# Three exponentials ahead of each pair of silus, GpSimd's products no longer held, and chunk 1's first fills spread: a Mamba + SwiGLU kernel

## The chip, the cores and the metric

One core of one Trainium2 chip. The metric is device time in microseconds (us) of one execution, the median of the runs shown; lower is better.

## The reference

The layer is a Mamba block and a SwiGLU block, each followed by a layer norm over a residual sum. The input has 4 sequences of 2048 tokens, model width 256; the inner width is 512, with 16 states per channel.

```python
x_in, res = jnp.split(x @ W_in, 2, axis=-1)
x_conv = silu(_causal_dw_conv(x_in, conv_w, conv_b))
dt, Bm, Cm = jnp.split(x_conv @ W_x, [DT_RANK, DT_RANK + N_STATE], axis=-1)
delta = softplus(dt @ W_dt + b_dt);  A = -exp(A_log)
def step(h, inp):            # along time, for each channel and state
    dA_i, dBu_i, C_i = inp   # exp(delta*A), delta*B*u, C
    h = dA_i * h + dBu_i
    return (h, einsum('bdn,bn->bd', h, C_i))
x = layernorm(x + (y + x_conv * D) * silu(res) @ W_out)
x = layernorm(x + (silu(x @ wg.T) * (x @ wu.T)) @ wd.T)
```

## The kernel before

The 8192 tokens are cut into 16 chunks of 512. Chunk after chunk, a step of 64 **beats** runs the selective scan: beat `b` handles state `b // 4` of channel block `b % 4`, a tile of 128 channels by 512 tokens. A beat needs three things: ScalarE's exponential `da` (function `exp`, line 1094), GpSimd's product `dbu` = `du` times `brep` (`times_b`, line 1237), and VectorE's scan over them (`scan`, line 1432), which makes `h`. TensorE turns `h` to tokens by channels in two halves (`turn_upper`, `turn_lower`, line 737). ScalarE weighs the upper half by C into `gt` (`weigh`, line 1103) and TensorE turns that back into `y_upper` (line 762); VectorE sums the lower half into `acc` (line 1444). The bank `ht_upper` is free for TensorE's next turn only when `gt` is read from it.

All else is fitted between the beats. While chunk i is scanned, the front of chunk i+1 (`xin`, `conv`, `res`, `dtb`, `ct`, `dt`) and the back of chunk i-1 (`o`, `x1t`, `gate`, `up`, `down`) run: TensorE's **fills** into two spare banks at the beats of the table `FILL_AT`, and the reads of them at the beats of `READ_AT`. A table `BEAT` places the rest. Each engine's queue is in the order of these beats, and runs in order; semaphores tie the queues. Chunk 1's front runs in step 0 at beats of its own (`EARLY_FILL`, `EARLY_READ`).

Silu and exponential lie in different tables of ScalarE, so the silus of a step are gathered in two **windows**, each between two table loads (lines 1167 and 1179). `BEAT["silu uz"]` = [31, 32]: the silu of u (next chunk) and of z. `BEAT["silu gate"]` = [43, 45]: the two halves of the gates' silu (line 993); the product with them is VectorE's `kb<-fill` (line 1354), one for each of `up0` to `up5`. Step 0 has z's silu in place of the gates'.

For the beats of a window the exponentials are made in front of it: `AHEAD` = 2 of them, for beats 32, 33 and 44, 45. They go to the buffer `da_ahead`, in SBUF, where all other `da` alternate between two PSUM banks and so wait for the scan two beats before. The exponential of the beat behind these comes after the window.

`HOLD` = (2, 3) delays one product of GpSimd for each window. A product normally waits for the scan four beats before it (`DBU` = 4 buffers). Product 34 waits for the scan of beat 33 instead of 30, and product 47 for beat 45 instead of 43:

```python
used = beat - DBU if beat >= DBU else max(b for b in range(NH) if b % DBU == beat) - NH
after(pool, h_ready, i * NH + max(used, HELD.get(beat, used)) + 1)
```

Scans of most beats have one tile operand in PSUM (`da`) and one in SBUF (`dbu`); those of a window have both in SBUF.

Of the kernel before, what the change touches and what calls it, by code (L numbers as in the profile page):

```python
# [45 lines left out]
FILL_BANKS = 2  # L46


EARLY_FILL = {"xin0": (0, 0), "xin1": (1, 1), "xin2": (2, 2), "xin3": (3, 3), "conv0": (5,), "conv1": (8,),
              "conv2": (11,), "conv3": (14,)}  # L50
EARLY_READ = {"xin0": 1, "xin1": 2, "xin2": 3, "xin3": 4, "conv0": 7, "conv1": 10, "conv2": 13, "conv3": 16}

# [12 lines left out]
        "times u": [53, 59, 63, 63], "x1 cut": [30, 35], "x1 low": [29.5, 30.5], "y upper": [5.5, 6],  # L67
        "times z": [12, 12, 15, 17], "mean": [20.5, 73.5], "rstd": [25.5, 83], "shift": [27, 83],
        "square": [(21, 21, 21, 23), (79.5, 79.5, 82, 82)], "norm": [(27, 27, 27, 27), (96, 103, 108, 108)],
        "halo": -17.5, "silu uz": [31, 32], "silu gate": [43, 45]}  # L70
FIRST_FILLS = ["xin0", "xin1", "xin2", "xin3", "conv2", "conv0", "conv1", "conv3", "dtb", "dt0", "dt1", "ct", "dt2", "dt3"]

FIRST_RES = ["o0", "o1", "o2", "o3"]
# [9 lines left out]
FIRST_BANKS = FILL_BANKS + 4  # L83
assert sorted(FIRST_FILLS + ["res0", "res1", "res2", "res3"]) == sorted(F_FILLS)
STORE_AT = max(int(BEAT["norm"][1][-1]) + 1 - 64, 0)
AHEAD = 2
DBU = 4
HOLD = (2, 3)

SILUS = sorted(int(BEAT[name][0]) for name in ("silu uz", "silu gate"))  # L90
assert all(start <= BEAT[name][1] <= int(start) + AHEAD + 0.5 for name in ("silu uz", "silu gate") for start in BEAT[name][:1])
assert not [at for kind in ("soft exp", "soft ln", "rstd") for at in BEAT[kind] for start, end in (BEAT["silu uz"], BEAT["silu gate"])
            if start < at % 64 <= end]
SAVE_AT = 3
assert all(b - a > AHEAD + 1 for a, b in zip(SILUS, SILUS[1:]))

assert all(len(at) == TT and at[-1] <= BEAT["rstd"][n] for n, at in enumerate(BEAT["square"]))
AFTER_SILU = [start + AHEAD + 1 for start in SILUS]

HELD = {start + 1 + HOLD[n]: start + AHEAD for n, start in enumerate(SILUS) if HOLD[n]}  # L100
assert all(last < product < 64 and product - last <= DBU for product, last in HELD.items())
# [8 lines left out]
def fill_at(c, name):  # L110

    return EARLY_FILL[name] if c == 1 and name in EARLY_FILL else FILL_AT[name]


def read_at(c, name):

    return EARLY_READ[name] if c == 1 and name in EARLY_READ else READ_AT[name]

# [34 lines left out]
def mamba_swiglu(nc, x, x_t, w_in, conv_w, conv_b, w_x, w_dt, b_dt, a_log, d_skip, w_out, w_gate_t, w_up_t,  # L153
# [30 lines left out]
    with ExitStack() as ctx:  # L184
        def sb(name, shape, dt=F32):
            return ctx.enter_context(nc.sbuf_tensor(name, shape, dt))
# [36 lines left out]
        dbu = sb("dbu", [P, DBU, T])  # L223
        da_ahead = sb("da_ahead", [P, AHEAD, T])

# [114 lines left out]
        def ahead(beat):  # L340

            for start in SILUS:
                if start < beat <= start + AHEAD:
                    return beat - start - 1
# [1255 lines left out]
```

How the kernel before makes its waits and increments, by code:

```python
        def after(eng, semaphore, value):  # L318
            if not isinstance(value, int) or value > 0:
                eng.wait_ge(semaphore, value)
# [42 lines left out]
        def wait_tail(eng, name):  # L364
            eng.wait_ge(tail_filled, list(TAIL).index(name) + 1)
# [17 lines left out]
        @block.sync  # L383
# [10 lines left out]
            def store(c, par):  # L394
                sp.wait_ge(o_ready, TT * (c + 1))
                sp.dma_start(tokens(out_flat, c * (T * DM)), xr[:, par, :, :]).then_inc(out_stored, 16)
# [1 line left out]
            def shift_xin(c, m):  # L398
                if m == 0 or isinstance(c, int) and c == 0:
                    sp.wait_ge(xin_ready, c * (DB + 1) + (m + 2))
                else:
                    sp.wait_ge(*filled(c, f"conv{m - 1}"))
                for k in range(0, KCONV, 2 if isinstance(c, int) and c == 0 else 1):
                    sp.dma_start(tap_rows(c, m, slice(k, P, KCONV)), xin[:, m, k:k + T])\
                        .then_inc(first_loaded[m] if isinstance(c, int) and c == 0 else xs_loaded, 16)
# [28 lines left out]
            sp.dma_start(wx_s[:, :, XB:XB + NS], w_x_v[:, :, R:R + NS]).then_inc(small_loaded, 16)  # L438
            sp.dma_start(wx_s[:, :, XC:XC + NS], w_x_v[:, :, R + NS:R + 2 * NS]).then_inc(small_loaded, 16)
            sp.wait_ge(wdt_zero, 1)
            sp.dma_start(wdt_s[0:R, :], w_dt).then_inc(small_loaded, 16)
# [4 lines left out]
                shift_xin(0, m)  # L446
            sp.wait_ge(xt_loaded, 16)
            load_xt(1)
# [3 lines left out]
            write_b(0)
            sp.wait_ge(b_written, 16)
            spread_b(0, 1)
```

## Time and profile before

| | |
|---|---|
| median of 3 runs | 1827.73 us (1825.76 to 1829.15) |
| the profiled execution: own time, span | 1828.88 us, 1827.1 us |
| TensorE (PE) busy | 1692.4 us, 93% |
| VectorE (DVE) busy | 1683.2 us, 92% |
| ScalarE (ACT) busy | 1602.9 us, 88% |
| GpSimd (POOL) busy | 1605.0 us, 88% |
| mean granted TensorE clock | 0.993 |

The span is the time from the first to the last instruction. Busy time is the union of an engine's instructions; PEld is TensorE's weight load. All four engines are busy for about nine tenths, so the averages do not tell which one a stretch waits for; the timeline of one step does. The pattern of a step repeats every 108.8 us from step 1 to step 14, to a few hundredths of a microsecond. Idle time on an engine is given in the rows in brackets, with what ended it.

### The profile page before, as it was taken

How to read it: one execution, taken by the hardware profiler on the slowest of the kernel's cores; microseconds unless marked ns; L12 is line 12 of the kernel's file. 1: busy time of each engine (PE TensorE's matmuls, PEld its weight loads, DVE VectorE, ACT ScalarE, POOL GpSimd, SP SyncE). 2: the span in 40 equal slices, each digit the busy share in tenths (PEclk: the TensorE clock that was granted, in tenths of full speed). 3: DMA queues.
4: the chain of work that ended last, by engine and by line, in shares of the span. 5: the costliest groups of instructions: out<-in, count | busy, mean ns of one | idle time of the engine just before them, and what ended most of it. 6: DMA issues, size and time to landing. Idle time of an engine off the chain costs nothing.

```text
span 1827.1 us, 32557 instructions
## 1 busy us (share of the span) xinstructions
PE 1692.4 (93%) x10128; PEld 1272.1 (70%) x10128; DVE 1683.2 (92%) x1958; ACT 1602.9 (88%) x2769; POOL 1605.0 (88%) x1629
## 2 busy tenths in 40 slices
PE   7869898998989999898999989899898999988788
PEld 3547676776767677676776767677676777767667
DVE  4899999999999999999999999999999999999994
ACT  4797989989898998989899898998989899898874
POOL 2889799998999899899998989999898998989870
PEclk9999999999999999999999999999999999999999
DMA  7212213232222322323222222313222232221110
GB/s 241 104 59 104 80 61 116 79 119 71 105 92 71 116 71 105 105 77 109 82 105 82 104 82 82 114 62 128 81 82 104 82 115 72 105 71 58 36 47 24
DMA packets 82108, 164.57 MB, mean 90 GB/s; under 512 B 10369, under 2 KB 28033, under 8 KB 81938
## 3 DMA queue, kind: packets, MB, share of 16 engines
q1 hardware_dynamic: 80498, 160.90, 25.6%
q8 instruction: 85, 1.39, 0.3%
q10 hardware_dynamic: 1440, 1.58, 0.3%
q14 instruction: 85, 0.70, 0.1%
HBM read 87.47 MB, written 8.91 MB: 53 GB/s over the span
## 4 chain that ended last, share of the span: by engine, by line
PE 74%; ACT 14%; POOL 5%; issue 4%; DVE 2%; DMA 1%; SPq 0%; DVEq 0%; ACTq 0%; POOLq 0%
PE ht_upper L737 11%; PE ht_lower L737 10%; PE y_upper L762 9%; PE fill L663 8%; PE fill L673 8%; PE fill L559 7%; PE fill L642 6%; POOL dbu L1237 4%; PE fill L612 3%; PE fill L595 3%; PE fill L574 3%; ACT da L1094 2%; ACT gt L1103 2%; DVE h L1432 2%; ACT z L988 1%
## 5 line engine op out<-in xcount | busy, mean ns | idle before, releaser
L1237 POOL TENSOR_TENSOR dbu<-du,brep 128x512 f32<-128x512 f32 x1024 | 1284.7, 1285 | 157.5 <-DVE h L1432 133.6
L1432 DVE TENSOR_TENSOR_SCAN h<-da,carry,dbu 128x512 f32<-128x512 f32 x960 | 1185.2, 1269 | 62.9 <-ACT da L1094 58.3
L1094 ACT ACTIVATE da<-delta,a_s 128x512 f32<-128x512 f32 x960 | 654.7, 692 | 78.7 <-DVE h L1432 71.5
L1103 ACT ACTIVATE gt<-ht_upper,ct 128x512 f32<-128x512 f32 x512 | 349.5, 683 | 68.9 <-PE ht_upper L737 65.8
L737 PE MATMUL ht_upper<-ident,h 128*128 128x128 f32 x2048 | 315.7, 277 | 73.4 <-ACT gt L1103 45.0
L737 PEld LDWEIGHTS ht_upper<-ident,h 128*128 128x128 f32 x2048 | 243.7, 142 | 196.4 <-issue 131.2
L1444 DVE SCALAR_TENSOR_TENSOR acc<-ht_lower,ct,acc 128x512 f32<-128x512 f32 x480 | 350.0, 729 | 9.0 <-PE ht_lower L737 7.6
L737 PE MATMUL ht_lower<-ident,h 128*128 128x128 f32 x2048 | 312.5, 275 | 25.7 <-DVE acc L1444 21.9
L762 PE MATMUL y_upper<-ident,gt 128*128 128x128 f32 x2048 | 309.6, 274 | 0.5 <-ACT kb L920 0.5
L737 PEld LDWEIGHTS ht_lower<-ident,h 128*128 128x128 f32 x2048 | 239.8, 142 | 79.0 <-DVE h L1432 37.1
L762 PEld LDWEIGHTS y_upper<-ident,gt 128*128 128x128 f32 x2048 | 246.0, 142 | 51.3 <-issue 38.2
L559 PE MATMUL fill<-xt_s,win_s 128*128 128x512 f32 x456 | 224.8, 601 | 11.8 <-DVE x1t L1365 11.8
L673 PE MATMUL fill<-wd_s,kb 128*128 128x256 f32 x720 | 177.7, 380 | 0.0
L673 PEld LDWEIGHTS fill<-wd_s,kb 128*128 128x128 f32 x720 | 127.4, 190 | 18.3 <-issue 6.7
L642 PE MATMUL fill<-wout_s,kb 128*128 128x256 f32 x480 | 122.4, 383 | 0.7 <-DVE xr L1343 0.7
L559 PEld LDWEIGHTS fill<-xt_s,win_s 128*128 128x128 f32 x456 | 75.1, 192 | 55.5 <-issue 55.5
L663 PE MATMUL fill<-x1t,wu_s 128*128 128x512 f32 x360 | 110.4, 435 | 0.4 <-DVE kb L1354 0.4
L663 PE MATMUL fill<-x1t,wg_s 128*128 128x512 f32 x360 | 107.1, 419 | 0.0
L642 PEld LDWEIGHTS fill<-wout_s,kb 128*128 128x128 f32 x480 | 85.3, 190 | 21.3 <-issue 12.8
L663 PEld LDWEIGHTS fill<-x1t,wu_s 128*128 128x128 f32 x360 | 64.9, 191 | 23.8 <-issue 6.7
L1432 DVE TENSOR_TENSOR_SCAN h<-da_ahead,carry,dbu 128x512 f32<-128x512 f32 x64 | 80.2, 1275 | 0.0
L1354 DVE SCALAR_TENSOR_TENSOR kb<-fill,kb 128x512 f32<-128x512 f32 x90 | 61.5, 683 | 19.3 <-PE fill L663 19.2
(189 smaller groups left out, 1876.2 us busy)
## 6 DMA issues: line engine op xcount, KB each, us to landing
brep<-b_rows SPq DMA_DIRECT2D x127, 512.0 KB, 3.8
xs<-xin SPq DMA_DIRECT2D x242, 256.0 KB, 2.5
xr<-x SPq DMA_DIRECT2D x16, 512.0 KB, 5.5
xt_s<-x_t SPq DMA_DIRECT2D x15, 512.0 KB, 3.8
out<-xr SPq DMA_DIRECT2D x15, 512.0 KB, 2.9
win_s<-w_in SPq DMA_DIRECT2D x2, 512.0 KB, 5.4
h<-xin SPq DMA_DIRECT2D x4, 256.0 KB, 3.9
h<-xin ACTq DMA_DIRECT2D x4, 256.0 KB, 4.6
```

The source lines that it names most:

```text
L559: mm = nc.tensor.matmul(front_bank(c, name)[:, :], win_s[:, k, m * P:(m + 1) * P], xt_place(c)[:, k, :], start=(k == 0), stop=(k == KK - 1))
L642: mm = nc.tensor.matmul(fill_bank(name)[:, 0:DM], kb[:, m, t * P:(t + 1) * P], wout_s[:, m, :], start=(m == 0), stop=(m == DB - 1))
L663: mm = nc.tensor.matmul(fill_bank(name)[:, :], w[:, k, n * P:(n + 1) * P], x1t[:, half, k, :], start=(k == 0 and half == 0), stop=(k == KK ...
L673: mm = nc.tensor.matmul(fill_bank(name)[:, 0:DM], kb[:, n, t * P:(t + 1) * P], wd_s[:, n, :], start=(n == 0), stop=(n == HB - 1))
L737: mm = nc.tensor.transpose(bank[:, m * P:(m + 1) * P], h[:, n % 2, m, t * P:(t + 1) * P], ident[:, :])
L762: mm = nc.tensor.matmul(y_upper[m // 2][:, (m % 2) * HALF + k * P:(m % 2) * HALF + (k + 1) * P], lhsT=gt[:, (n * UPPER + k) % GT, m * P:(m ...
L1094: nc.scalar.activation(dst[:, :], delta[:, par, m, :], ACT.Exp, scale=a_s[:, m, n:n + 1])\
L1103: nc.scalar.activation(gt[:, (n * UPPER + k) % GT, :], ht_upper[:, :], ACT.Copy, scale=ct[:, par, k, n:n + 1])\
L1237: nc.gpsimd.tensor_tensor(dbu[:, beat % DBU, :], du[:, par, m, :], brep[:, n // PIECE % 2, n % PIECE, :], ALU.mult).then_inc(dbu_ready, 1)
L1354: nc.vector.scalar_tensor_tensor(out=kb[:, m, :], in0=fill_bank(name)[:, :], scalar=W_SCALE, in1=kb[:, m, :], op0=ALU.mult, op1=ALU.mult)\
L1432: nc.vector.tensor_tensor_scan(h[:, n % 2, m, 0:T], da[beat % 2][:, :] if slot is None else da_ahead[:, slot, :], dbu[:, beat % DBU, :], c ...
L1444: nc.vector.scalar_tensor_tensor(out=acc[:, par, k, :], in0=ht_lower[:, :], scalar=ct[:, par, UPPER + k, n:n + 1], in1=acc[:, par, k, :], ...
```

## The change

`AHEAD` goes from 2 to 3 and `silu uz` starts at beat 30.5: beats 31, 32, 33 and 44, 45, 46 have their exponentials in `da_ahead`. `HOLD` becomes (0, 0): no product waits longer than for its buffer. The fills of chunk 1's front, which in step 0 stood at beats 0 to 14, stand at beats 1 to 27.

```diff
-EARLY_FILL = {"xin0": (0, 0), "xin1": (1, 1), "xin2": (2, 2), "xin3": (3, 3), "conv0": (5,), "conv1": (8,),
-              "conv2": (11,), "conv3": (14,)}
-EARLY_READ = {"xin0": 1, "xin1": 2, "xin2": 3, "xin3": 4, "conv0": 7, "conv1": 10, "conv2": 13, "conv3": 16}
+EARLY_FILL = {"xin0": (1, 1), "xin1": (2, 4), "xin2": (1, 6), "xin3": (9, 9), "conv0": (7,), "conv1": (13,),
+              "conv2": (20,), "conv3": (27,)}
+EARLY_READ = {"xin0": 1, "xin1": 6, "xin2": 8, "xin3": 12.5, "conv0": 10, "conv1": 14, "conv2": 23, "conv3": 29.5}
...
-        "halo": -17.5, "silu uz": [31, 32], "silu gate": [43, 45]}
+        "halo": -17.5, "silu uz": [30.5, 32], "silu gate": [43, 45]}
...
-AHEAD = 2
+AHEAD = 3
...
-HOLD = (2, 3)
+HOLD = (0, 0)
```

ScalarE at the second window of steps 1 to 15, before (`L993` is the gates' silu, `L957` a copy of the next chunk's `dtb`):

```order
229 L1094 ACTIVATE da<-delta,a_s 128x512 x2
230 L1094 ACTIVATE da_ahead<-delta,a_s 128x512 x2
231 L1167 ACT_TABLE_LOAD
232 L993 ACTIVATE kb<-kb 128x1536
233 L1103 ACTIVATE gt<-ht_upper,ct 128x512
234 L957 ACTIVATE xd<-fill,consts 128x512
235 L993 ACTIVATE kb<-kb 128x1536
236 L1179 ACT_TABLE_LOAD
237 L1094 ACTIVATE da<-delta,a_s 128x512
238 L1103 ACTIVATE gt<-ht_upper,ct 128x512
```

and with the change:

```order
228 L1094 ACTIVATE da<-delta,a_s 128x512 x2
229 L1094 ACTIVATE da_ahead<-delta,a_s 128x512 x3
230 L1167 ACT_TABLE_LOAD
231 L993 ACTIVATE kb<-kb 128x1536
232 L1103 ACTIVATE gt<-ht_upper,ct 128x512
233 L957 ACTIVATE xd<-fill,consts 128x512
234 L993 ACTIVATE kb<-kb 128x1536
235 L1179 ACT_TABLE_LOAD
236 L1094 ACTIVATE da<-delta,a_s 128x512
237 L1103 ACTIVATE gt<-ht_upper,ct 128x512
```

One exponential, that of beat 46, moved from behind the second table load to in front of the first; the silus and the `gt` between them stand one exponential later.

VectorE at the two windows of step 1, as a difference (`x1t` is the low part of the cut layer-norm output):

```order
 L1432 SCALAR_TENSOR_TENSOR h<-da0,carry,dbu 128x512
 L1365 TENSOR_TENSOR x1t<-fill1,kb 128x512
-L1432 SCALAR_TENSOR_TENSOR h<-da1,carry,dbu 128x512
+L1432 SCALAR_TENSOR_TENSOR h<-da_ahead,carry,dbu 128x512
 L1444 SCALAR_TENSOR_TENSOR acc<-ht_lower,ct,acc 128x512
 L1432 SCALAR_TENSOR_TENSOR h<-da_ahead,carry,dbu 128x512 x2
...
 L1444 SCALAR_TENSOR_TENSOR acc<-ht_lower,ct,acc 128x512
 L1354 SCALAR_TENSOR_TENSOR kb<-fill1,kb 128x512
-L1432 SCALAR_TENSOR_TENSOR h<-da0,carry,dbu 128x512
+L1432 SCALAR_TENSOR_TENSOR h<-da_ahead,carry,dbu 128x512
 L1432 SCALAR_TENSOR_TENSOR h<-da1,carry,dbu 128x512
```

The order of VectorE's queue is the same; one scan more in each window (beats 31 and 46) reads its exponential from SBUF instead of a PSUM bank.

TensorE at the start of step 0, where `L559` fills chunk 1's `xin` and `L574` its `conv`:

```order
-L559 MATMUL fill0<-kb,win_s 128x512 x4
-L559 MATMUL fill1<-kb,win_s 128x512 x4
-L737 MATMUL ht_upper<-ident,h 128x128 x4
-L737 MATMUL ht_lower<-ident,h 128x128 x4
+L559 MATMUL fill1<-kb,win_s 128x512
+L559 MATMUL fill0<-kb,win_s 128x512 x3
+L737 MATMUL ht_upper<-ident,h 128x128 x4
+L737 MATMUL ht_lower<-ident,h 128x128 x4
+L559 MATMUL fill0<-kb,win_s 128x512
+L737 MATMUL ht_upper<-ident,h 128x128 x4
+L559 MATMUL fill1<-kb,win_s 128x512
+L737 MATMUL ht_lower<-ident,h 128x128 x4
```

All eight `xin` matmuls stood in front of the first turn of `h`; now four do, and one each stands behind the turns that follow. GpSimd's queue has the same order as before; only what products 34 and 47 wait for is different. In the queue that issues DMAs, one load of `brep` now stands between the first and the second group of chunk 1's `xs` loads, and another in front of the fourth.

## Rows read from the trace of the kernel before

**Rows 1.** Page, engines' busy time, share of span, instructions
```profile
PE 1692.4 (93%) x10128; PEld 1272.1 (70%) x10128; DVE 1683.2 (92%) x1958; ACT 1602.9 (88%) x2769; POOL 1605.0 (88%) x1629
```
**Rows 2.** Waits of the whole span: us in total, times, longest
```profile
DVE h L1432 <- ACT da L1094: 58.3, 71, 2.3
```
**Rows 3.** Timeline, VectorE, step 8's first window: start, duration, instruction [idle before <-releaser]
```profile
961.19 1.27 DVE L1432 TENSOR_TENSOR_SCAN h<-da,carry,dbu 128x512 f32<-128x512 f32 x1
...
963.02 2.45 DVE L1432 TENSOR_TENSOR_SCAN h<-da_ahead,carry,dbu 128x512 f32<-128x512 f32 x2
...
968.48 2.47 DVE L1432 TENSOR_TENSOR_SCAN h<-da,carry,dbu 128x512 f32<-128x512 f32 x2 [2.32 <-ACT da L1094]
```
**Rows 4.** Timeline, ScalarE, same window
```profile
957.89 0.64 ACT L920 ACTIVATE x1t<-kb 128x512 fp32r<-128x512 f16 x1
958.41 0.70 ACT L1094 ACTIVATE da<-delta,a_s 128x512 f32<-128x512 f32 x1
...
967.75 0.69 ACT L1094 ACTIVATE da<-delta,a_s 128x512 f32<-128x512 f32 x1
```
**Rows 5.** Timeline, VectorE, step 8's second window
```profile
985.82 0.69 DVE L1354 SCALAR_TENSOR_TENSOR kb<-fill,kb 128x512 f32<-128x512 f32 x1 [0.65 <-PE fill L663]
...
987.95 0.69 DVE L1354 SCALAR_TENSOR_TENSOR kb<-fill,kb 128x512 f32<-128x512 f32 x1 [0.24 <-PE fill L663]
...
989.82 2.45 DVE L1432 TENSOR_TENSOR_SCAN h<-da,carry,dbu 128x512 f32<-128x512 f32 x2
```
**Rows 6.** Timeline, ScalarE, second window
```profile
981.00 1.32 ACT L1094 ACTIVATE da_ahead<-delta,a_s 128x512 f32<-128x512 f32 x2
...
985.02 0.67 ACT L1103 ACTIVATE gt<-ht_upper,ct 128x512 f32<-128x512 f32 x1
...
988.95 0.69 ACT L1094 ACTIVATE da<-delta,a_s 128x512 f32<-128x512 f32 x1
```
**Rows 7.** Timeline, TensorE, second window
```profile
985.83 0.63 PE L737 MATMUL ht_upper<-ident,h 128*128 128x128 f32 x4
```
**Rows 8.** Timeline, GpSimd, both windows
```profile
961.08 1.27 POOL L1237 TENSOR_TENSOR dbu<-du,brep 128x512 f32<-128x512 f32 x1
...
981.55 2.51 POOL L1237 TENSOR_TENSOR dbu<-du,brep 128x512 f32<-128x512 f32 x2
987.79 1.28 POOL L1237 TENSOR_TENSOR dbu<-du,brep 128x512 f32<-128x512 f32 x1 [3.73 <-DVE h L1432]
```
**Rows 9.** Timeline, GpSimd and VectorE where both read two SBUF tiles, step 0
```profile
30.80 0.69 DVE L1507 TENSOR_TENSOR du<-delta,u 128x512 f32<-128x512 f32 x1
32.27 1.27 POOL L1237 TENSOR_TENSOR dbu<-du,brep 128x512 f32<-128x512 f32 x1 [20.06 <-DVE brep L1513]
32.73 1.36 DVE L1507 TENSOR_TENSOR du<-delta,u 128x512 f32<-128x512 f32 x1
90.73 2.51 POOL L1237 TENSOR_TENSOR dbu<-du,brep 128x512 f32<-128x512 f32 x2
92.84 2.65 DVE L1432 TENSOR_TENSOR_SCAN h<-da_ahead,carry,dbu 128x512 f32<-128x512 f32 x2
```
**Rows 10.** Timeline, step 0, beats 3 to 35: GpSimd, ScalarE, VectorE
```profile
39.17 6.15 POOL L1237 TENSOR_TENSOR dbu<-du,brep 128x512 f32<-128x512 f32 x5 [1.23 <-DVE du L1507]
40.98 0.60 ACT L920 ACTIVATE xin<-fill 128x512 f32<-128x512 f32 x1 [2.48 <-PE fill L559]
...
89.83 2.45 DVE L1432 TENSOR_TENSOR_SCAN h<-da,carry,dbu 128x512 f32<-128x512 f32 x2
97.58 2.47 DVE L1432 TENSOR_TENSOR_SCAN h<-da,carry,dbu 128x512 f32<-128x512 f32 x2 [0.53 <-ACT da L1094]
```
**Rows 11.** Groups, GpSimd: busy us, mean ns of one
```profile
L1295 POOL COPY carry<-h 128x4 f32<-128x4 f32 x255 | 50.4, 198 | 0.0
...
L1250 POOL TENSOR_SCALAR wd_s<-wd_s 128x512 f32<-128x512 int32 x3 | 4.5, 1491 | 0.0
...
L1246 POOL CAST wg_s<-kb 128x512 fp32r<-128x512 int32 x3 | 1.8, 613 | 0.0
```

## The prediction

> **What bounds the kernel now.** I read the engines' shares first: TensorE 93%, VectorE 92%, the others 88% [rows 1]. They name no bound. So I read the waits of the scan, which paces a step: VectorE waits 58.3 us in all for exponentials [rows 2]. Then the timeline of step 8, which steps 1 to 14 repeat.
>
> In the first window VectorE stands idle 2.32 us in front of the scan of beat 34 [rows 3]. ScalarE's queue is the cause, and it has no hole: the cut of `x1t` at 957.89, the exponential of beat 31 at 958.41, and so on to the exponential of beat 34, 967.75 + 0.69 = 968.44; the scan starts at 968.48 [rows 3, 4]. In the second window no scan waits for an exponential: the one of beat 46 is there at 988.95 + 0.69 = 989.64, and its scan starts at 989.82, directly behind VectorE's own work [rows 5, 6]. What VectorE waits for there is TensorE's up fills, 0.65 and 0.24 us [rows 5].
>
> **Part 1, the third exponential, second window.** The exponential of beat 46 is wanted no earlier, so its move gains nothing. What it costs: two exponentials fill 981.00 to 982.32, the last of them at full length, so one more takes about 1.32 - 0.70 = 0.62 us [rows 4, 6]. The table load, the silus and the `gt` between them are 0.62 later. That `gt` frees `ht_upper`: it ends at 985.02 + 0.67 = 985.69, and TensorE's turn starts at 985.83, only 0.14 behind [rows 6, 7]. TensorE's queue runs in order, and behind this turn stand the fills `up1` and `up2`. VectorE already waits 0.24 for `up1` at 987.95, so the whole 0.62 lands there [rows 5]. Nothing behind it takes it back: TensorE goes on without a hole, and ScalarE does the same work. **+0.62 per step** in steps 1 to 15; the exponential leaves the far side of the window, but what is late there is TensorE. Bounds: 0.5 (some of it hidden) and 0.75.
>
> **Part 2, the third exponential, first window.** ScalarE's queue has the same work in the same order. Only the exponential of beat 31 goes to SBUF and so need not wait for the scan of beat 29. It did not wait: it starts 0.52 behind a cut of 0.64, at the pace of overlapping copies [rows 4]. Gain 0, and the 2.32 us stall stays. If it had waited, a whole scan would be the most, about 1.2.
>
> **Part 3, no product held.** GpSimd idles 3.73 us for the second window's hold [rows 8], but no scan of steps 1 to 14 waits for a product, so freeing it gains nothing directly. What it may cost shows in step 0. A VectorE product of two SBUF tiles takes 0.69 alone; the next, started at 32.73 while GpSimd runs a product from 32.27 to 33.54, takes 1.36: it ends 0.69 behind 33.40, so it stood until GpSimd was nearly through [rows 9]. Two scans from `da_ahead`, begun at 92.84 under a product that ends at 93.24, take 2.65 against 2.45 [rows 3, 9]. **A VectorE instruction with two SBUF tiles waits for a GpSimd product that began first.** The scans of a window are such instructions; the holds kept GpSimd still beside them, and the change adds one of them per window and takes the holds away.
>
> The Trainium skill says so too (SBUF — State Buffer, Who interferes with whom): a VectorE instruction with two SBUF inputs contends with a GpSimd instruction that reads SBUF, and whichever issues first blocks the other. Rows 9 agree in one direction, GpSimd first. Without this rule the sum below would be about +1 us, with it +7; both are worked out from rows here.
>
> First window, walked with step 8's times. Scan 31 is due at 961.19, product 33 runs from 961.08 to 962.35 [rows 3, 8]: scan 31 works from about 962.2 and is 1.0 late. Product 34, free now, gets in behind it, and scan 32 is due at 964.0 with product 34 until 964.5: 0.4 more. Product 35 may get in once more, 1.0. Together 2.4, against the 2.32 that VectorE idles anyway: **+0.1 per step**. Bounds: 0, and 1.4, if each of the three scans waits a full 1.25.
>
> Second window: scan 44 begins as products 45 and 46 end (981.55 + 2.51 [rows 8]). Product 47 stands behind scan 44, and whether product 48 or scan 45 is first at 986.4 is a tie; a wait of 1.0 there is nearly covered by the 0.24 + 0.62 for `up1`. **+0.1 per step.** Bounds 0 and 1.1.
>
> **Part 4, chunk 1's fills spread.** Early in step 0 VectorE waits for ScalarE and ScalarE for TensorE's `xin` fills, as the 2.48 in front of 40.98 shows [rows 10]. With the fills and reads apart these waits go. The next thing late is GpSimd. From 39.17 (product 3) to product 30 its queue holds 28 products, six casts of `wg`/`wu`, three scalings of `wd`, six carries: 28 x 1.23 + 6 x 0.61 + 3 x 1.49 + 6 x 0.2 = 34.4 + 3.7 + 4.5 + 1.2 = 43.8 [rows 10, 11]. Scan 30 can start at 83.1; before it was 89.83 [rows 10]: 6.7 gained. The queue is tight at the first window then, so scans 31 to 33 and products 32 to 34 take turns, one of 1.2 behind the other: scan 34 at about 91.6 against 97.58 [rows 10]: 6.0. In the second window of step 0 a scan stands behind product 47, and I give back 0.5. **-5.5 for step 0.** Bounds: -8.3 (no collision, the window's waits gone too) and -3.5 (half of the gain lost to new waits on `conv1` and `res` fills around beats 13 to 19). The loads of `brep` that change places in the DMA queue wait for products 8 and 16, which come in front of their new neighbours; nothing.
>
> **Sum.** -5.5 + 14 x (0.62 + 0.1 + 0.1) = -5.5 + 11.5, and for the last step, where the first window idles less, 1.3: **+7.3 us**. The profiled execution took 1828.88 us, so 1836.2; the median of the runs shown is 1.15 lower. I forecast **1835.0**. With the bounds of each part mixed, this case lies between 1830 and 1844.
>
> **The rivals.**
> *No collisions* (slower and faster parts cancel). If GpSimd and the scans pass each other, step 0 gains 8.5 and each of 15 steps loses 0.64 (part 1, and 0.02 for one exponential more that is written to SBUF): +1.1, so 1828.8. For it: the median scan from `da_ahead` is not longer; against it: those scans had GpSimd held. It decides if the scans of the windows stay at 1.27. Chance 0.20.
> *The free exponential pays* (the other side). If the exponential of beat 31 did wait for scan 29, ScalarE's queue of the first window starts up to 1.2 earlier, and the 2.32 stall shrinks by that: 0.82 - 1.2 = -0.4 per step, -5.7 over 15, and -5.5 for step 0: 1816.5. If instead the `gt` does not set TensorE's turn, part 1 is 0 and the sum is 7.3 - 15 x 0.62 = -2.0, 1825.7. It decides where a hole on ScalarE shows before 958.41, or one of more than 0.6 before TensorE's 985.83; rows 4 show none, rows 7 show 0.14. Chance 0.13.
> *GpSimd first each time.* All scans of both windows wait a whole product: 0.62 + 1.4 + 1.1 = 3.1 for 15 steps, less 3.5: +43, 1871. For it: GpSimd's next product is always ready when a scan ends. Against it: it can be four beats ahead at most, and then waits itself. Chance 0.07.
>
> **Numbers.** My forecast has 0.60. A measurement of this kernel tells 0.2%, 3.7 us, from no change. Slower by more: 0.55 of my case, 0.07, and a little of the first rival, 0.64. Within 0.2%: 0.04 and most of the first rival, 0.20. Faster: 0.16. The range leaves out the heavy rival and most of the faster one: 1825.5 to 1844.
>
> **What would show it.** Right: in steps 1 to 14 scans from `da_ahead` of 1.4 to 2.4 us where a product runs; a period of about 109.6 instead of 108.8; the wait for `up1` grown from 0.24 to about 0.8; the first window's stall for beat 34 shrunk, without time gained; step 0 about 5.5 shorter. Wrong: `da_ahead` scans all near 1.27, a turn behind the silu's `gt` that does not move, or a first window that is shorter from scan 30 to scan 34.

## The result, and the profile after

The changed kernel takes 1839.18 us (median of 4 runs, 1835.41 to 1840.77), the kernel before 1828.44 beside it (4 runs, 1825.76 to 1829.27). The ratio is 1.006, with a 95% interval of 1.0046 to 1.0074: slower by 0.6%, about 10.7 us. The forecast was 1835.0, the range 1825.5 to 1844.0. The profiled execution took 1839.47, its span is 1837.7, against 1828.88 and 1827.1 before; the granted clock is 0.990 of full speed, against 0.993. So the two profiles differ by 10.6 as well, and can be used to place the loss, with one caution: each has short stretches in which TensorE's granted clock is half of full speed, and they do not lie at the same places. Behind the last step's first silu table load the granted clock is 0.97 before and 0.93 after.

The page's busy times after the change, to set beside [rows 1]:

```profile
PE 1699.3 (92%) x10128; PEld 1273.6 (69%) x10128; DVE 1735.0 (94%) x1958; ACT 1603.9 (87%) x2769; POOL 1654.7 (90%) x1629
```

TensorE and ScalarE do the same work in nearly the same time. VectorE is busy for 52 us more and GpSimd for 50 us more, with the same number of instructions. The groups of the page say which ones became longer (busy us, mean ns of one, idle time before):

```profile
L1432 DVE TENSOR_TENSOR_SCAN h<-da_ahead,carry,dbu 128x512 f32<-128x512 f32 x96 | 177.0, 1857 | 0.0
```

The scans that read their exponential from SBUF take 1857 ns in the mean, where the 64 of before took 1275. Their number grew by half, and their time more than doubled, from 80.2 to 177.0 us. So "busy" here holds waiting: an instruction that has begun and stands is counted as work. The views of waits don't show it at all. They look better than before: VectorE's wait for exponentials, to be set beside [rows 2], is down from 58.3 us to 19.9.

```profile
DVE h L1432 <- ACT da L1094: 19.9, 45, 1.2
```

The loss itself is placed by ScalarE's first silu table load of a step, which comes once per step at the same place. Timeline of ScalarE after the change, the loads of steps 0, 1, 8, 9 and 15 (start, duration):

```profile
84.71 1.28 ACT L1167 ACT_TABLE_LOAD   x1
...
195.16 1.28 ACT L1167 ACT_TABLE_LOAD   x1
...
961.87 1.28 ACT L1167 ACT_TABLE_LOAD   x1
...
1071.36 1.28 ACT L1167 ACT_TABLE_LOAD   x1
...
1732.23 1.28 ACT L1167 ACT_TABLE_LOAD   x1
```

The kernel before has them here:

```profile
91.28 1.28 ACT L1167 ACT_TABLE_LOAD   x1
...
197.43 1.28 ACT L1167 ACT_TABLE_LOAD   x1
...
960.37 1.28 ACT L1167 ACT_TABLE_LOAD   x1
...
1069.16 1.28 ACT L1167 ACT_TABLE_LOAD   x1
...
1724.59 1.28 ACT L1167 ACT_TABLE_LOAD   x1
```

At step 0's window the change is 6.6 us ahead (91.28 - 84.71); at step 1's only 2.3 (197.43 - 195.16). From there to step 15's window it takes 1537.07 where before took 1527.16, so 9.9 more in 14 steps: the step from 961.87 to 1071.36 is 109.49 long against 108.79, 0.70 more. Behind step 15's window lie 105.5 against 102.5, 3.0 more. The sum is -2.3 + 9.9 + 3.0 = 10.6.

Now step 8 in detail. Timeline of VectorE, first window, after the change (beside [rows 3]):

```profile
960.93 1.27 DVE L1432 TENSOR_TENSOR_SCAN h<-da,carry,dbu 128x512 f32<-128x512 f32 x1
...
962.70 3.50 DVE L1432 TENSOR_TENSOR_SCAN h<-da_ahead,carry,dbu 128x512 f32<-128x512 f32 x1
...
966.77 3.05 DVE L1432 TENSOR_TENSOR_SCAN h<-da_ahead,carry,dbu 128x512 f32<-128x512 f32 x2
...
970.39 2.44 DVE L1432 TENSOR_TENSOR_SCAN h<-da,carry,dbu 128x512 f32<-128x512 f32 x2
```

And GpSimd there:

```profile
962.63 2.49 POOL L1237 TENSOR_TENSOR dbu<-du,brep 128x512 f32<-128x512 f32 x2
966.28 1.28 POOL L1237 TENSOR_TENSOR dbu<-du,brep 128x512 f32<-128x512 f32 x1 [1.16 <-DVE h L1432]
967.51 1.12 POOL L1295 COPY carry<-h 128x4 f32<-128x4 f32 x1
```

Scan 31, now from SBUF, begins at 962.70, 0.07 behind products 33 and 34, which end at 965.12. It is done at 966.20: a scan of 1.27 would then have begun at 964.9, so it stood through both products. Scan 32 begins at 966.77 under product 35 and stands as well, which makes the pair 3.05 instead of 2.45. GpSimd stands in its turn: the copy of the carry, which takes 0.19 before, takes 1.12 here and ends at 968.63, when the first scan of the pair ends. VectorE's stall of 2.32 for the exponential of beat 34 is gone altogether, because VectorE is late itself: scan 34 starts 0.4 behind its exponential.

The second window, VectorE (beside [rows 5]):

```profile
987.56 0.69 DVE L1354 SCALAR_TENSOR_TENSOR kb<-fill,kb 128x512 f32<-128x512 f32 x1 [0.86 <-PE fill L663]
988.16 2.09 DVE L1432 TENSOR_TENSOR_SCAN h<-da_ahead,carry,dbu 128x512 f32<-128x512 f32 x1
990.17 0.66 DVE L1354 SCALAR_TENSOR_TENSOR kb<-fill,kb 128x512 f32<-128x512 f32 x1
...
992.01 1.27 DVE L1432 TENSOR_TENSOR_SCAN h<-da_ahead,carry,dbu 128x512 f32<-128x512 f32 x1
```

ScalarE and TensorE there (beside [rows 6, 7]):

```profile
982.54 1.95 ACT L1094 ACTIVATE da_ahead<-delta,a_s 128x512 f32<-128x512 f32 x3
...
987.19 0.67 ACT L1103 ACTIVATE gt<-ht_upper,ct 128x512 f32<-128x512 f32 x1
...
991.12 0.69 ACT L1094 ACTIVATE da<-delta,a_s 128x512 f32<-128x512 f32 x1
```

```profile
988.00 0.63 PE L737 MATMUL ht_upper<-ident,h 128*128 128x128 f32 x4 [0.56 <-ACT gt L1103]
```

Three exponentials take 1.95 where two took 1.32, 0.63 more. The `gt` ends at 987.86, and TensorE's turn follows 0.14 behind, as before. Scan 45 takes 2.09: it meets product 48. And no wait for `up1` is left in front of 990.17. From the profile alone one cannot tell whether the late `gt` or the collision of scan 45 is what the step pays for. Each could be hidden by the other. That is what the experiments had to settle.

### The profile page after: what moved, and what is told of

Same layout as the page of the kernel before. It is cut to its first block, busy times and chain, and to the rows that moved or that the text cites. A ratio compares the mean times of both kernels' runs of the same rounds, so it can differ in the third digit from the quotient of the medians.

```text
span 1837.7 us, 32557 instructions
## 1 busy us (share of the span) xinstructions
PE 1699.3 (92%) x10128; PEld 1273.6 (69%) x10128; DVE 1735.0 (94%) x1958; ACT 1603.9 (87%) x2769; POOL 1654.7 (90%) x1629
## 3 DMA queue, kind: packets, MB, share of 16 engines
q10 hardware_dynamic: 1440, 1.58, 0.3%
## 4 chain that ended last, share of the span: by engine, by line
PE 67%; ACT 15%; POOL 9%; issue 5%; DVE 3%; DMA 0%; SPq 0%; DVEq 0%; ACTq 0%; POOLq 0%
PE ht_upper L737 10%; PE ht_lower L737 9%; PE y_upper L762 9%; PE fill L673 8%; PE fill L663 8%; PE fill L559 7%; POOL dbu L1237 7%; PE fill L642 5%; PE fill L612 3%; ACT da_ahead L1094 2%; ACT gt L1103 2%; PE fill L574 2%; ACT L1167 2%; DVE h L1432 2%; ACT da L1094 1%
## 5 line engine op out<-in xcount | busy, mean ns | idle before, releaser
L1237 POOL TENSOR_TENSOR dbu<-du,brep 128x512 f32<-128x512 f32 x1024 | 1313.9, 1312 | 116.0 <-DVE h L1432 91.0
L1432 DVE TENSOR_TENSOR_SCAN h<-da,carry,dbu 128x512 f32<-128x512 f32 x928 | 1145.4, 1268 | 22.9 <-ACT da L1094 19.9
L1094 ACT ACTIVATE da<-delta,a_s 128x512 f32<-128x512 f32 x928 | 632.0, 693 | 78.8 <-DVE h L1432 72.8
L559 PE MATMUL fill<-xt_s,win_s 128*128 128x512 f32 x456 | 224.9, 601 | 11.7 <-DVE x1t L1365 11.7
L1432 DVE TENSOR_TENSOR_SCAN h<-da_ahead,carry,dbu 128x512 f32<-128x512 f32 x96 | 177.0, 1857 | 0.0
L559 PEld LDWEIGHTS fill<-xt_s,win_s 128*128 128x128 f32 x456 | 75.2, 192 | 55.6 <-issue 55.6
```

The lines of the kernel that those rows point to most:

```text
L559: mm = nc.tensor.matmul(front_bank(c, name)[:, :], win_s[:, k, m * P:(m + 1) * P], xt_place(c)[:, k, :], start=(k == 0), stop=(k == KK - 1))
L1094: nc.scalar.activation(dst[:, :], delta[:, par, m, :], ACT.Exp, scale=a_s[:, m, n:n + 1])\
L1237: nc.gpsimd.tensor_tensor(dbu[:, beat % DBU, :], du[:, par, m, :], brep[:, n // PIECE % 2, n % PIECE, :], ALU.mult).then_inc(dbu_ready, 1)
L1432: nc.vector.tensor_tensor_scan(h[:, n % 2, m, 0:T], da[beat % 2][:, :] if slot is None else da_ahead[:, slot, :], dbu[:, beat % DBU, :], c ...
```

## The experiments

All ran beside the kernel before on the same chip; the ratios are to it. A step's period is read from the table loads, as above; 108.79 is that of before. It is the period of most steps, not of all: in the kernel before the loads of steps 5 and 6 lie 108.78 apart, those of steps 4 and 5 109.79, those of steps 11 and 12 110.16. In such a long step TensorE's `conv` fill stands waiting for a DMA (`xs<-xin`), 1.06 us at 626.54 and 1.15 at 1389.67, and VectorE waits behind it. Every profile has one to three of these, so the period of the undisturbed steps tells a small difference better than the time of one run.

**1. The fills alone.** The kernel before with both tables of chunk 1's fills from the change.

```diff
-EARLY_FILL = {"xin0": (0, 0), "xin1": (1, 1), "xin2": (2, 2), "xin3": (3, 3), "conv0": (5,), "conv1": (8,),
-              "conv2": (11,), "conv3": (14,)}
-EARLY_READ = {"xin0": 1, "xin1": 2, "xin2": 3, "xin3": 4, "conv0": 7, "conv1": 10, "conv2": 13, "conv3": 16}
+EARLY_FILL = {"xin0": (1, 1), "xin1": (2, 4), "xin2": (1, 6), "xin3": (9, 9), "conv0": (7,), "conv1": (13,),
+              "conv2": (20,), "conv3": (27,)}
+EARLY_READ = {"xin0": 1, "xin1": 6, "xin2": 8, "xin3": 12.5, "conv0": 10, "conv1": 14, "conv2": 23, "conv3": 29.5}
```

> Before, with chunk 1's fills spread alone (two exponentials ahead, holds 2 and 3). Theory (GpSimd's queue is next in step 0, and steps 1 to 15 are untouched): scan 30 of step 0 near 83.8 instead of 89.83, the whole kernel 5 to 7 us faster, 1822 +- 1.5, and the period of steps 1 to 14 stays 108.8. Rival A (the spread gains only the 3.7 us that step 0 gained in the changed kernel, whatever is held): 1824.7. Rival B (the fills gain nothing that is kept at the end of step 0): 1828.

Measured: 1825.21 us (12 runs, 1820.12 to 1828.76), ratio 0.9982, interval 0.9973 to 0.9991. VectorE in step 0's first window:

```profile
87.13 2.45 DVE L1432 TENSOR_TENSOR_SCAN h<-da_ahead,carry,dbu 128x512 f32<-128x512 f32 x2
...
91.87 2.47 DVE L1432 TENSOR_TENSOR_SCAN h<-da,carry,dbu 128x512 f32<-128x512 f32 x2 [0.53 <-ACT da L1094]
```

Scan 34 stands at 91.87, 5.7 ahead of before [rows 10]. At the first scan of step 1 only 3.4 of it is left (144.95 against 148.31). That need not be the spread's doing: from scan 34 to there the granted clock is 0.92 in this profile and 0.97 before; experiment 8, also spread and at 0.97 there, keeps its 4.9 (scan 34 at 92.71, the first scan of step 1 at 143.42). In step 1 something else is lost. TensorE's `conv` fill waits for a DMA:

```profile
188.26 1.07 PE L574 MATMUL fill<-xs,taps 128*32 128x512 f32 x8 [1.35 <-DMA xs<-xin]
```

VectorE waits 1.47 at 190.39 for TensorE behind it. All five profiles with the fills spread have this wait in step 1 (1.3 to 1.6 us on VectorE), and in the eight others it is 0.21 at most. So it comes with the spread; how the spread makes the DMA late is not shown. By the medians the spread is worth 3.4 us (interval 1.6 to 4.9): the theory's 1822 misses, and the first rival's 1824.7 is near. The profiled run was the slowest of the twelve, 1828.76, so its total shows nothing of the gain.

**2. The holds alone.** The kernel before with `HOLD = (0, 0)`.

```diff
-HOLD = (2, 3)
+HOLD = (0, 0)
```

> Before, with the holds gone alone (two exponentials ahead, fills as before). Theory (a scan with two SBUF operands stands behind GpSimd's products as long as these follow one another): the scans of beats 32 and 33 are blocked, hidden under the 2.32 us that VectorE idles there; scan 45 takes about 2.0 us instead of 1.27 with only 0.24 us of cover, so about +0.5 per step, +7 us, 1835. Rival C (collisions in the second window are covered by the wait for up1, as in the changed kernel, and the exponential is the whole loss): within 1 us of before.

Measured: 1835.88 us (5 runs, 1833.92 to 1839.27), ratio 1.0043, interval 1.0031 to 1.0055; the period is 109.46. VectorE in step 8, both windows:

```profile
965.96 4.08 DVE L1432 TENSOR_TENSOR_SCAN h<-da_ahead,carry,dbu 128x512 f32<-128x512 f32 x2
...
971.39 2.47 DVE L1432 TENSOR_TENSOR_SCAN h<-da,carry,dbu 128x512 f32<-128x512 f32 x2 [0.71 <-ACT da L1094]
...
989.36 2.29 DVE L1432 TENSOR_TENSOR_SCAN h<-da_ahead,carry,dbu 128x512 f32<-128x512 f32 x1
991.57 0.66 DVE L1354 SCALAR_TENSOR_TENSOR kb<-fill,kb 128x512 f32<-128x512 f32 x1
```

The first window's pair loses 1.6 (4.08 against 2.45), and the stall behind it shrinks by as much (2.32 to 0.71): no time. Scan 45 loses 1.0, of which the wait of 0.24 for `up1` and a little more is covered: 0.67 per step. Theory and time agree. So the missing holds alone cost as much per step as the whole change does.

**3 and 4. Three exponentials, with both products held.** The kernel before with three exponentials and `HOLD = (3, 3)`, and the changed kernel with the same holds: product 34 waits for scan 33, as before, and product 47 for scan 46, one scan longer than before.

```diff
-AHEAD = 2
-HOLD = (2, 3)
+AHEAD = 3
+HOLD = (3, 3)
-"silu uz": [31, 32]
+"silu uz": [30.5, 32]
```

```diff
-HOLD = (0, 0)
+HOLD = (3, 3)
```

> Before, with three exponentials ahead from beat 30.5 alone; product 34 held for the scan of beat 33 and product 47 for that of beat 46, fills as before. Theory (the later gt delays TensorE's turn, up1 and VectorE): period 109.45, +0.65 for 15 steps, about +9.5 us, 1838. Rival D (the loss comes from the holds that were dropped, the exponential is free): period 108.8, 1828.

> The changed kernel, with the two products held as in the run before. Theory: step 0 no longer loses the 4.3 us scan of beat 31 entirely (product 34 waits), so 2 to 3 us are won there, and steps 1 to 14 keep 109.45: 1835 to 1837. Rival D (dropped holds are the loss): period back to 108.8 and 1828 or less.

Measured: 1886.42 us (4 runs, ratio 1.0317, interval 1.0304 to 1.033) and 1882.01 (5 runs, ratio 1.029, interval 1.0277 to 1.0303). Both theories miss by far. GpSimd, then VectorE, behind the second window of the first of the two:

```profile
1021.23 1.28 POOL L1237 TENSOR_TENSOR dbu<-du,brep 128x512 f32<-128x512 f32 x1 [7.02 <-DVE h L1432]
```

```profile
1022.60 1.28 DVE L1432 TENSOR_TENSOR_SCAN h<-da,carry,dbu 128x512 f32<-128x512 f32 x1 [1.45 <-issue]
...
1054.12 2.51 DVE L1432 TENSOR_TENSOR_SCAN h<-da,carry,dbu 128x512 f32<-128x512 f32 x2 [1.22 <-issue]
```

Product 47 waits for scan 46, and GpSimd idles 7.02 us instead of 3.73. Scan 47 then has to wait for it, 1.45 us. 32 us later a scan waits 1.22 with nothing that the profile names, most likely for its product again. The period is 112.5. These two runs don't price the exponential; they show that behind the second window GpSimd has little room beyond what the hold of before used. One number of them counts: VectorE's wait for `up1`, at 1018.01, is 0.85.

**5. The third exponential in the second window alone,** with the holds of before (product 34 until scan 33, product 47 until scan 45).

```diff
-AHEAD = 2
+AHEAD = 3
+AHEADS = (2, 3)
...
-                if start < beat <= start + AHEAD:
+                if start < beat <= start + AHEADS[SILUS.index(start)]:
...
-HELD = {start + 1 + HOLD[n]: start + AHEAD for n, start in enumerate(SILUS) if HOLD[n]}
+HELD = {34: 33, 47: 45}
...
-                    for b in range(beat + 1, beat + 1 + AHEAD):
+                    for b in range(beat + 1, beat + 1 + AHEADS[SILUS.index(beat)]):
...
-                        exp(i, par, int(start) + AHEAD + 1)
+                        exp(i, par, int(start) + AHEADS[SILUS.index(int(start))] + 1)
```

> The kernel before, with a third exponential in front of the second window's silus only; the first window has two as before, the fills stand as before, and product 34 waits for scan 33 and product 47 for scan 45, both as before (not for scan 46, the hold that cost 58 us in the last runs). Theory (the silu's gt is 0.62 later, so TensorE's turn and the up fills behind it are, and VectorE waits for up1): +0.62 in each of 15 steps, 1828.5 + 9.3 = 1837.8, period 109.4, the wait in front of VectorE's kb of up1 grown from 0.24 to about 0.85, scan 45 at 1.27. Rival (the exponential is free, and the whole +0.69 of the changed kernel is the collision of scan 45 with a product): 1828.5, period 108.8.

Measured: 1849.73 us (5 runs, 1844.54 to 1852.1), ratio 1.0113, interval 1.0098 to 1.0129; period 110.22. VectorE, step 8's second window:

```profile
995.39 1.28 DVE L1433 TENSOR_TENSOR_SCAN h<-da_ahead,carry,dbu 128x512 f32<-128x512 f32 x1
...
1000.04 0.69 DVE L1355 SCALAR_TENSOR_TENSOR kb<-fill,kb 128x512 f32<-128x512 f32 x1 [0.81 <-PE fill L664]
...
1001.90 2.37 DVE L1433 TENSOR_TENSOR_SCAN h<-da_ahead,carry,dbu 128x512 f32<-128x512 f32 x1
```

The wait for `up1` has grown from 0.24 to 0.81, as expected, and scan 46 stands 6.51 behind scan 44 where it stood 5.92 before: 0.59. But it is from SBUF now, and GpSimd, released by its hold, runs products 47 to 49 back to back: scan 46 loses another 1.1. The forecast of the run missed that, and with it the time.

**6. The same, with the `gt` of beat 43 issued in front of the exponentials.**

```diff
-"silu gate": [43, 45]
+"silu gate": [43.5, 45]
```

> As the last one, and the gt at beat 43 is issued in front of the three exponentials and the table load instead of behind them. Theory (the gt is the path): the turn is 1 us and more earlier than in the kernel before, no wait for up1 is left, and the period is 108.6 (the 0.24 gained, some of it found again at another wait): 1825 to 1828.5. Rival (the third exponential costs through ScalarE's later silus or a later table load, not through the gt): 1837, as without the gt moved.

Measured: 1843.55 us (4 runs, 1841.81 to 1846.07), ratio 1.0082, interval 1.0068 to 1.0096; period 109.99. The wait for `up1` is gone, but another has grown in front of the `kb` of `up0`, and scan 46 still collides. VectorE in step 7:

```profile
881.93 0.69 DVE L1355 SCALAR_TENSOR_TENSOR kb<-fill,kb 128x512 f32<-128x512 f32 x1 [1.16 <-ACT kb L994]
...
885.71 1.91 DVE L1433 TENSOR_TENSOR_SCAN h<-da_ahead,carry,dbu 128x512 f32<-128x512 f32 x1
```

That wait was 0.65 for TensorE; now it is 1.16 for the silu, which stands behind the `gt` and the three exponentials: 0.5 more. The theory misses: once the `gt` is out of the way, the silu is the next thing that is late. That is the rival's way, but not its time (1837), and the run does not isolate it: of the 1.2 per step, scan 46's collision is another 0.6, and scan 0 waits 0.40 with nothing that the profile names, as in experiment 9 below.

**7. The third exponential in the first window alone,** holds as before.

```diff
-"silu uz": [31, 32]
+"silu uz": [30.5, 32]
...
-AHEAD = 2
+AHEAD = 3
+AHEADS = (3, 2)
...
```

The rest is as in experiment 5.

> The kernel before, with three exponentials in front of the first window's silus only (31, 32, 33, from the middle of beat 30); the second window has two, fills as before, product 34 waits for scan 33 and product 47 for scan 45. Theory (the exponential of beat 31 did not wait for its buffer, so nothing on ScalarE starts earlier; scan 31 from SBUF waits 1.0 for a product, under an idle time of 2.3 that is there anyway): 1828.5 within 1.0, period 108.8, the stall for exponential 34 shorter by about 1. Rival (the freed exponential pays): 1811 to 1822. Other rival (the collision of scan 31 comes through): 1843.

Measured: 1829.43 us (11 runs, 1825.49 to 1832.09), ratio 1.0008, interval 0.9998 to 1.0017; period 108.79, no change. VectorE there:

```profile
962.71 2.27 DVE L1433 TENSOR_TENSOR_SCAN h<-da_ahead,carry,dbu 128x512 f32<-128x512 f32 x1
...
969.99 2.47 DVE L1433 TENSOR_TENSOR_SCAN h<-da,carry,dbu 128x512 f32<-128x512 f32 x2 [1.35 <-ACT da L1095]
```

Scan 31 loses 1.0 behind one product, the stall shrinks from 2.32 to 1.35, and scan 34 starts where it would have. Part 2 of the prediction holds: the exponential did not pay, and theory and time agree.

**8. The fills spread and the `gt` first,** two exponentials, holds as before: the tables of experiment 1 and the edit of experiment 6.

> A candidate: the kernel before with chunk 1's fills spread (alone 1825.2) and the gt of beat 43 issued in front of the two exponentials of the second window. Theory: the wait of 0.24 for up1 goes in each step, up to 15 x 0.24 = 3.6 less: 1821.6; if the exponentials, now 0.67 later, or the silus make VectorE wait instead, 1825 or some more. Rival (the gt is not the path): 1825.2.

Measured: 1820.49 us (5 runs, 1818.85 to 1820.98), ratio 0.9954, interval 0.994 to 0.9967; period 108.59. The theory's 1821.6 holds. It beats both kernels.

**9. Experiment 5 with product 49 held too.**

```diff
-HELD = {34: 33, 47: 45}
+HELD = {34: 33, 47: 45, 49: 46}
```

> As the kernel with the third exponential in the second window only, and product 49 also waits for scan 46 (in that run products 47, 48 and 49 stood back to back and scan 46 took 2.37 us). Theory (a collision and the late gt are two costs that add there: 0.6 for the gt and 1.1 for scan 46 in a row of 1.43 per step): scan 46 back at 1.3, the wait for up1 at 0.8 as there, period 109.4, time 1837.5 within 1.5. Rival (the extra 0.8 per step is GpSimd running late behind its hold, not the collision): period 110 or more, 1846 and above.

Measured: 1843.13 us (5 runs, 1842.61 to 1845.8), ratio 1.009, interval 1.0076 to 1.0103; period 109.92. VectorE:

```profile
996.13 0.69 DVE L1355 SCALAR_TENSOR_TENSOR kb<-fill,kb 128x512 f32<-128x512 f32 x1 [0.85 <-PE fill L664]
...
997.99 1.28 DVE L1433 TENSOR_TENSOR_SCAN h<-da_ahead,carry,dbu 128x512 f32<-128x512 f32 x1
...
1029.63 2.51 DVE L1433 TENSOR_TENSOR_SCAN h<-da,carry,dbu 128x512 f32<-128x512 f32 x2 [0.37 <-issue]
```

The collision is gone and the wait for `up1` stays, yet the period is 0.5 longer than the theory's 109.4. At 1029.63 a scan starts 0.37 late with nothing that the profile names; the product that it needs is the first of four that GpSimd begins at 1028.22, which at 1.25 each ends at about 1029.5. The time misses both theories, 1837.5 and 1846, and lies between them: of the 1.43 of experiment 5, 0.6 is the late `gt`; the other 0.8 goes with the collision, and holding the collision away saves only 0.3 of it. The other 0.5 is back as a late start of the next step; that GpSimd's queue causes it is argued from the product's end, not isolated.

**10. The changed kernel without the long collisions.** Product 34 waits for scan 31, product 48 for scan 45.

```diff
-HELD = {start + 1 + HOLD[n]: start + AHEAD for n, start in enumerate(SILUS) if HOLD[n]}
+HELD = {34: 31, 48: 45}
```

> The changed kernel, with product 34 waiting for scan 31 and product 48 for scan 45. Theory: scan 31, at 3.50 us behind products 33 and 34, waits for product 33 alone and takes 2.3; the silus' exponential hides that, so no time is gained in the first window. Scan 45 takes 1.27 instead of 2.09, and a wait for up1 of about 0.8 appears in its place, since the gt is as late as it was: period 109.45 as in the changed kernel, time 1839 within 1.5. Rival (the collisions are the loss, and the late gt is not): period 108.8, time 1829.

Measured: 1834.06 us (5 runs, 1832.97 to 1836.99), ratio 1.0037, interval 1.0024 to 1.005; period 109.40 to 109.41. VectorE, both windows of step 8:

```profile
961.58 2.28 DVE L1432 TENSOR_TENSOR_SCAN h<-da_ahead,carry,dbu 128x512 f32<-128x512 f32 x1
...
964.42 4.02 DVE L1432 TENSOR_TENSOR_SCAN h<-da_ahead,carry,dbu 128x512 f32<-128x512 f32 x2
...
986.85 1.28 DVE L1432 TENSOR_TENSOR_SCAN h<-da_ahead,carry,dbu 128x512 f32<-128x512 f32 x1
988.97 0.69 DVE L1354 SCALAR_TENSOR_TENSOR kb<-fill,kb 128x512 f32<-128x512 f32 x1 [0.84 <-PE fill L663]
```

GpSimd in the first window:

```profile
963.94 3.42 POOL L1237 TENSOR_TENSOR dbu<-du,brep 128x512 f32<-128x512 f32 x2 [1.16 <-DVE h L1432]
```

This settles the question of the second window. Scan 45 is back at 1.28, and in its place stands the wait for `up1`, 0.84. The period barely moves, from 109.49 to 109.40. With the collision taken away the late `gt` costs 0.61 per step; with two exponentials and the collision alone (experiment 2) the step costs 0.67; both together cost 0.70. **They overlap and are not a sum.** The distance from scan 43 to scan 47 says the same without the rest of the step: 8.92 before, 9.53 here, 9.60 in experiment 2, 9.59 in the changed kernel.

In the first window scan 31 goes from 3.50 to 2.28, as it has one product in front of it and not two, but the pair behind it takes 4.02 instead of 3.05. Here scans and products do take turns: scan 32, begun at 964.42 under product 34, gets in when that ends at 965.21, and product 35 stands, 2.19 us long; so the two products take 3.42. No time comes of all this: from scan 30 to scan 43 it is 22.69 us, as in the changed kernel, and 22.67 before.

The period agrees with the theory, the time does not (1839 expected). The run is 5 us better than the changed kernel. In the profiles most of it lies in the last step: behind its first silu table load lie 101.5 us instead of 105.5. Of these 4.0 only 0.8 are seen in the first window (scan 34 stands 8.6 behind scan 30 instead of 9.45); the granted clock behind that load is 0.97 here and 0.93 there, and the rest may be that.

**11. The `gt` first, alone.** The kernel before with the edit of experiment 6.

> The kernel before, with the gt of beat 43 issued in front of the second window's exponentials and nothing else changed. Theory (TensorE's turn follows that gt, and VectorE's 0.24 for up1 follows the turn): the turn no longer waits for the gt, the wait for up1 is gone, period 108.59 as in the candidate that also spreads the fills, so 14 x 0.2 = 2.8 less and the same once more in the last step: 1825 within 1.5. Rival (the gain of the candidate over the spread alone came from step 0 or the last step, not from the gt): 1828.

Measured: 1821.97 us (6 runs, 1820.36 to 1824.87), ratio 0.9962, interval 0.9949 to 0.9975; period 108.54 to 108.56. TensorE in step 8's second window:

```profile
981.40 1.49 PE L663 MATMUL fill<-x1t,wu_s 128*128 128x512 f32 x4
982.73 0.60 PE L737 MATMUL ht_upper<-ident,h 128*128 128x128 f32 x4
```

The turn stands directly behind the fill before it, where it waited for the `gt`. The wait of 0.24 for `up1` is gone, and one of 0.31 three beats later as well; a part is taken back, as scan 46 now starts at 986.87, only 0.03 behind the end of its exponential. The step is 0.24 shorter, as forecast, 3.4 in 14 steps. The gain by the medians is 7 us (interval 4.6 to 9.3), so the time misses the theory, and where the rest comes from is not shown. The profiles put 2.7 of it into the last step (99.8 us behind its table load instead of 102.5), where the kernel before waits 2.45 us at the `kb` of `up1`. But the granted clock is 0.79 around that wait (from 1745 to 1753); in experiment 1, with the same code there and the clock at 1.00, the wait is 0.92. So most of the 2.7 can be the clock and not the `gt`. This run and number 8 have overlapping intervals, so what the spread adds to it is not settled.

## Why the prediction was right, and where it was not

The time, 1839.18, lies in the range, and the likeliest case came about. Part of the nearness is luck: the misses below have both signs and cancel in part. Point by point:

**Part 1, the third exponential, second window: right.** Forecast +0.62 per step through `gt`, TensorE's turn and `up1`. Experiment 10 shows it by itself: +0.61, with the wait for `up1` at 0.84, as the prediction had it (about 0.8). Experiment 11 shows the same chain from the other side. What part 1 didn't see is what experiment 6 shows: a silu stands close behind the `gt`, and is late next.

**Part 2, first window: right.** Experiment 7 measures nothing (interval -0.02% to +0.17%), and the stall of 2.32 goes to 1.35 without time gained.

**Part 3, no product held: the mechanism right, its walk wrong in one place.** The prediction let scans and products "take turns", each scan waiting for the rest of one product: 1.0, 0.4 and 1.0. The trace has 2.2 for scan 31 and 0.6 for the pair behind it. The sum of 2.8 is near the forecast 2.4, because scan 31 waits for two products and scan 32 then meets less. Taking turns is not wrong everywhere: in experiment 10 scan 32 does. In steps 1 to 14 the collisions were paid from the stall: from scan 30 to scan 43 the change takes 22.69 us against 22.67, where +0.1 was forecast. In the second window the prediction added 0.1 for the collision to the 0.62; the collision took 0.82, `up1`'s wait covered it, and scan 47 stands 0.67 farther behind scan 43. The sum of a regular step, 0.82, came out at 0.70. The prediction took step 8 for all of steps 1 to 14; the steps in which TensorE waits for `xs` are longer, before and after.

**Part 4, the spread: mis-sized.** Scan 30 of step 0 was forecast at 83.1 and stands at 83.80. But not all that went was the fills' doing: the kernel before has two stretches at half clock in step 0 (0.94 from 34 to 90), and experiment 6, with the same fills and the clock at 1.00 from 34 to 88, has its scan 30 at 87.23 and not at 89.83. That GpSimd's queue sets scan 30's time after the change is not shown either: GpSimd was busy for 44.03 of the 45 us from 39 to 84, but the waits that VectorE has there, 3.7 us in seven pieces, are for exponentials in all but one. Then the wrong walk counts. VectorE and GpSimd in step 0's first window, after the change:

```profile
84.99 4.28 DVE L1432 TENSOR_TENSOR_SCAN h<-da_ahead,carry,dbu 128x512 f32<-128x512 f32 x1
...
93.44 2.44 DVE L1432 TENSOR_TENSOR_SCAN h<-da,carry,dbu 128x512 f32<-128x512 f32 x2
```

```profile
84.46 3.73 POOL L1237 TENSOR_TENSOR dbu<-du,brep 128x512 f32<-128x512 f32 x3
```

Scan 31 stands through three products, 3.0 us, and scan 34 starts at 93.44 and not at 91.6: 4.1 gained instead of 6.0. At step 1's first scan it is 3.7 (144.63 against 148.31), where 5.5 was forecast. Then TensorE waits in step 1:

```profile
187.96 1.07 PE L574 MATMUL fill<-xs,taps 128*32 128x512 f32 x8 [1.46 <-DMA xs<-xin]
```

VectorE waits 1.58 at 190.09 behind it, and this takes the gain to the 2.3 of the table loads, past the bound of -3.5. The prediction has no term for it; of the DMA queue it looked only at the loads of `brep` that change places, and put them at nothing.

**The last step: mis-sized.** Forecast +1.3, measured +3.0. There the first window has only 0.79 of stall to hide behind, and the two collisions, 2.2 and 0.6, come through: scan 34 stands 9.45 behind scan 30 instead of 7.49, 1.96 more. This part is firm: the six experiments whose first window is that of before have 7.49 to 7.56, whatever their clock, and experiment 10, where scan 31 does not wait for two products, has 8.6. The other 1.0 is not explained. Experiment 1 has the last step's code unchanged and still 100.8 us behind the table load, not 102.5, so single profiles differ there by more than that.

So the sum of +7.3 became +10.6: a regular step 0.12 too dear (-1.6), the spread 3.2 too good, the last step 1.7 too cheap. One slip in the text: the first rival gives step 0 a gain of 8.5, the bounds of part 4 one of 8.3; nothing hangs on it.

**The rivals.** "No collisions" is refuted by the mean of 1857 ns. "The free exponential pays" is refuted by experiment 7 in the first window and by experiment 10 in the second. "GpSimd first each time" had the mechanism of scan 31, which waits for both products that are ready, and overrated its cost: scans 32 and 33 lose 0.6 together, and most of the loss fell into stalls.

## What to carry to other kernels

When a VectorE scan of two SBUF tiles meets GpSimd's products, let the bound of the price be the whole run of products that GpSimd has ready, not one of them, and look for it in the duration of the scan: it appears as busy time, while the views of waits improve. Two delays that end at the same wait are not a sum, so undo each of them alone before you name a cause. Price the first and last step apart from the regular ones: they lack the stalls behind which a regular step hides a cost. And before you give a difference in one stretch of two profiles to the change, compare the granted clock there, and look for a third profile with the same code.

## What was not expected of the hardware

Several VectorE scans with two inputs in SBUF, begun while GpSimd's products ran back to back, were not let in between them: scan 31 took 2.28 us behind one product, 3.50 behind two and 4.28 behind three, against 1.27 alone. The second and third product began after the scan and still went first. It is not always so: scan 32 of experiment 10 got in behind the first of two products that were both ready, and the second stood. No run shows what decides between the two.

The other way round, GpSimd stood while scans ran: the copy of 0.19 took 1.12 and ended with the scan beside it, and the three products from 981.97 in experiment 10, which take 3.73 undisturbed, took 4.70 across one scan.

The scans that read their exponential from PSUM (`da`) show nothing of this: their mean is 1268 ns after the change and 1269 before.
